# Cross-attention on one core: the first two projections and the first query-weight product in whole float32, weights in 128-column tiles from two queues

## The chip, the core and the metric

The program runs on one core of one Trainium2 chip. The metric is the device time of one execution, in microseconds (us), median of three runs. PE is TensorE, DVE is VectorE, ACT is ScalarE, POOL is GpSimd; SP is the engine whose queue issues most transfers here.

## What is computed

```python
# x [2, 2048, 512], ctx_768 [2, 77, 384]; H = 8 heads, D = 512
Q = (img_embed @ Wq).reshape(B, -1, H, D).transpose(0, 2, 1, 3)
K = (sent_embed @ Wk).reshape(B, -1, H, D).transpose(0, 2, 1, 3)
V = (sent_embed @ Wv).reshape(B, -1, H, D).transpose(0, 2, 1, 3)
score = jnp.einsum('bhqd,bhkd->bhqk', Q, K) / math.sqrt(D)
mask = (atten_mask != 0)[:, None, None, :]
score = jnp.where(mask, score, -jnp.inf)
attn = jax.nn.softmax(score, axis=-1)
ctx = jnp.einsum('bhqk,bhkd->bqhd', attn, V).reshape(B, -1, H * D)
out = ctx @ Wo + img_embed
mu = jnp.mean(out, axis=-1, keepdims=True)
var = jnp.var(out, axis=-1, keepdims=True)
return (out - mu) * jax.lax.rsqrt(var + EPS) * gamma + beta
```

All inputs are float32. The kernel never forms Q or V at full size: for every head it multiplies the query weights with the keys (Wq Kᵀ, called `a`), and the values with the output weights (V Wo, called `vw`), both on the 2 x 77 = 154 context tokens, and then works row tile by row tile of x.

## The kernel before

**Two stages.** In the first, `u` runs over 16 uses, 8 heads of keys and then 8 heads of values. `project(u)` multiplies a 384 x 512 weight block (`w_proj`, from `wk` or `wv`) with the context: four output tiles `m` of 128, each the sum of three products (k = 0 to 2). `out_product(u)` multiplies a 512 x 512 block (`w_out`, from `wq_t` or `wo`) with that result: four tiles of four products. In the second stage 32 tiles of 128 rows of x pass through scores, softmax, transposition, output product and layer norm.

**Split operands.** The matmuls run on float32r, a float32 with fewer mantissa bits. To keep precision every operand is split: ACT rounds it (`..._hi`), DVE or POOL subtracts to get the rest (`..._lo`). `short_product` then makes hi x hi and hi x lo in one 308-column matmul (`w_hi` against 2 x 154 columns), and lo x hi in one 154-column matmul. So a product costs two matmuls, and each weight block is rounded once by ACT and subtracted once by another engine: `w_proj` on POOL (line 760; use 0 alone on DVE, line 565), `w_out` on DVE (line 582). The result of a projection is evicted by ACT (`round_kv`, line 477) and split by DVE in two steps (`split_kv`, lines 598 and 602).

**Order.** Every engine has a hand-written list. PE: 8 warm-up matmuls on zeros, `project(0)`, then for each u `project(u+1)` and `out_product(u)`. From u = 10 on some out-products have transpositions of `vw_t` in their middle (line 357). ACT: ctx, w_proj of use 0 in four tiles, w_proj of use 1, then per u `round_kv(u+1)`, `round_w_proj(u+2)`, half 0 of the out-product's eviction, `round_w_out(u+1)`, half 1. DVE: ctx, w_proj of use 0, the mask bias (lines 570 and 575, from a mask that ACT's queue loads first of all), then per u `split_kv(u+1)`, half 0 of the out-product, `split_w_out(u+1)`, half 1. POOL subtracts w_proj of uses 1 to 15 and is idle else.

**Transfers.** All weights come over SP's queue in order: ctx, four 128-column tiles of use 0, two halves of use 1, then w_out(0), w_proj(2), w_out(1), gamma, beta, and on from there, each block in one transfer into a ring of three, once PE has done with the block before it in the ring. A 128-column tile of w_proj is 128 x 3 pieces of 512 bytes in memory.

Of the kernel before, what the change touches and what calls it, by code (L numbers as in the profile page):

```python
# [40 lines left out]
class Shapes:  # L41


    def __init__(self, x_tiles, ctx_t, w_proj, w_out, mask):
# [7 lines left out]
        self.dim = w_proj.shape[3]  # L52
# [26 lines left out]
def build(nc, x_tiles, x_rows, ctx_t, wk, wq_t, wv, wo, mask, gamma, beta, out):  # L79
# [5 lines left out]
    WARM_UP = 8  # L85
# [4 lines left out]
    with ExitStack() as stack:  # L90
# [54 lines left out]
        with nc.sbuf_tensor("w_out_hi0", [P, s.dim_t, s.model], F32R) as w_out_hi0, \  # L145
# [3 lines left out]
        prob = [sb("prob0", [P, s.row]), prob1]  # L149
        assert 3 * s.row <= s.dim_t * s.model  # L150
# [21 lines left out]
        ld_second = [sem(f"ld_second{n}") for n in range(2)]  # L172
# [10 lines left out]
        act_ctx_hi, act_first_hi, act_p_hi, act_o_hi = sem("act_ctx_hi"), sem("act_first_hi"), sem("act_p_hi"), sem("act_o_hi")  # L183
# [3 lines left out]
        dve_mask, dve_ctx_lo, dve_first_lo, dve_o_lo = sem("dve_mask"), sem("dve_ctx_lo"), sem("dve_first_lo"), sem("dve_o_lo")  # L187
# [41 lines left out]
        def _(sp):  # L229
# [16 lines left out]
            def load_w_proj(u):  # L246
# [570 lines left out]
```

## Time and profile before

| | us |
|---|---|
| median of 3 runs (lowest, highest) | 376.74 (375.97, 378.13) |
| the profiled execution | 375.72 |
| its span in the trace | 373.9 |
| PE busy | 360.4 |
| DVE busy | 296.0 |

The profiled execution is 1.02 us under the median, and 1.8 us of it lie outside the span. All times below count from the start of the span. An entry such as "DVE w_out_lo L582" is an operation of DVE at line 582 that writes `w_out_lo`. The start of a row is where the engine took the instruction up; a wait inside the instruction is part of its duration.

### The profile page before, as it was taken

Reading aid. Unit: us, or ns where it says so; the run is one execution under the profiler, and the core shown is the slowest. Engines: PE = TensorE matmul, PEld = TensorE weight load, DVE = VectorE, ACT = ScalarE, POOL = GpSimd, SP = SyncE. Lnnn points to the kernel's source line nnn. Section 1 sums busy time; section 2 is a strip of 40 time slices with the busy share of each in tenths; the row PEclk is TensorE's granted clock in tenths of the full one; section 3 lists DMA queues with packets and bytes.
Section 4 is the critical chain, followed back from the end, with each engine's and each line's share of the span. In section 5 each row is a group of like instructions: output and inputs, shape, how many; then the busy total and the mean of one; then the engine's idle time right before and its main releaser. Section 6 shows DMA issues by size and latency. Waiting matters only on the chain.

```text
span 373.9 us, 6759 instructions
## 1 busy us (share of the span) xinstructions
PE 360.4 (96%) x2352; PEld 335.1 (90%) x2352; DVE 296.0 (79%) x483; ACT 215.7 (58%) x750; POOL 220.9 (59%) x195
## 2 busy tenths in 40 slices
PE   6899999999999999999999999999999999999991
PEld 3899999999999998999899889988998899899880
DVE  4799999988888577777877777777778777877796
ACT  4775775777676575654565466446644654564610
POOL 0564564464338112677677757776776677667555
PEclk9999999999999999999999999999999999999997
DMA  7997768865731400314233143142241340411012
GB/s 220 389 417 283 284 242 309 339 253 203 274 141 59 169 25 34 98 74 140 88 110 140 44 156 128 43 169 85 86 140 59 140 141 30 168 66 48 30 58 84
DMA packets 20642, 55.81 MB, mean 149 GB/s; under 512 B 1664, under 2 KB 4224, under 8 KB 18560
## 3 DMA queue, kind: packets, MB, share of 16 engines
q1 hardware_dynamic: 20464, 55.29, 41.2%
q8 instruction: 19, 0.31, 0.4%
q14 instruction: 15, 0.12, 0.1%
q10 hardware_dynamic: 144, 0.08, 0.1%
HBM read 46.98 MB, written 8.39 MB: 148 GB/s over the span
## 4 chain that ended last, share of the span: by engine, by line
PE 85%; DVE 6%; POOL 3%; ACT 2%; DMA 2%; issue 1%; SPq 1%; POOLq 0%
PE pair L372 28%; PE pair L398 26%; PE pair L305 26%; PE pair L384 4%; DVE w_out_lo L582 2%; DMA w_proj<-wk 2%; PE pair L357 1%; POOL out_sb L755 1%; ACT prob L506 1%; SPq L253 1%; DVE kv_t L602 1%; POOL var_eps L744 1%; POOL centred L751 1%; ACT w_out_hi L469 1%; DVE rest L598 1%
## 5 line engine op out<-in xcount | busy, mean ns | idle before, releaser
L506 ACT ACTIVATE prob<-masked,neg_max 128x77 f32<-128x77 f32 x256 | 88.3, 347 | 100.3 <-DVE neg_max L638 100.3
L760 POOL TENSOR_TENSOR w_proj_lo<-w_proj,w_proj_hi 128x768 fp32r<-128x768 f32 x30 | 55.1, 1859 | 59.3 <-ACT w_proj_hi L461 59.3
L305 PE MATMUL pair<-kv_t,w_out_hi 128*128 128x308 f32 x256 | 66.9, 334 | 0.0
L398 PE MATMUL pair<-vw_hi,pt_hi 128*128 128x512 f32 (+1 forms) x160 | 63.2, 395 | 0.0
L398 PE MATMUL pair<-vw_lo,pt_hi 128*128 128x512 f32 (+1 forms) x160 | 63.2, 395 | 0.0
L398 PE MATMUL pair<-vw_hi,pt_lo 128*128 128x512 f32 (+1 forms) x160 | 62.5, 391 | 0.0
L372 PE MATMUL pair<-a_hi,xt_hi 128*128 128x308 f32 x256 | 59.5, 314 | 0.0
L744 POOL TENSOR_SCALAR var_eps<-mean_var 128x1 f32<-128x1 f32 x32 | 24.2, 757 | 58.8 <-DVE mean_var L676 58.5
L372 PE MATMUL pair<-a_lo,xt_hi 128*128 128x308 f32 x256 | 57.1, 304 | 0.0
L372 PE MATMUL pair<-a_hi,xt_lo 128*128 128x308 f32 x256 | 57.0, 304 | 0.0
L737 POOL TENSOR_TENSOR xt_lo<-xt_in,xt_hi 128x512 fp32r<-128x512 f32 x32 | 44.0, 1376 | 20.6 <-ACT xt_hi L498 20.6
L582 DVE TENSOR_TENSOR w_out_lo<-w_out,w_out_hi 128x1024 fp32r<-128x1024 f32 x32 | 52.9, 1691 | 2.6 <-ACT w_out_hi L469 2.2
L305 PE MATMUL pair<-ctx_split,w_proj_hi 128*128 128x308 f32 x192 | 51.4, 339 | 3.4 <-ACT w_proj_hi L450 2.4
L305 PE MATMUL pair<-kv_t,w_out_lo 128*128 128x154 f32 x256 | 52.1, 245 | 0.0
L634 DVE TENSOR_TENSOR masked<-pair,mask_bias 128x616 f32<-128x616 f32 x32 | 25.6, 799 | 29.9 <-PE pair L372 29.9
L506 ACT ACTIVATION_READ_ACCUMULATOR prob<-masked,neg_max 128x1 f32 x256 | 48.0, 187 | 0.0
L305 PEld LDWEIGHTS pair<-kv_t,w_out_lo 128*128 128x128 f32 x256 | 45.5, 190 | 0.0
L305 PEld LDWEIGHTS pair<-kv_t,w_out_hi 128*128 128x128 f32 x256 | 45.0, 190 | 0.0
L755 POOL TENSOR_TENSOR out_sb<-centred,beta_sb 128x512 f32<-128x512 f32 x31 | 40.6, 1310 | 4.4
L372 PEld LDWEIGHTS pair<-a_hi,xt_lo 128*128 128x128 f32 x256 | 42.3, 189 | 0.0
L372 PEld LDWEIGHTS pair<-a_lo,xt_hi 128*128 128x128 f32 x256 | 42.2, 188 | 0.0
L372 PEld LDWEIGHTS pair<-a_hi,xt_hi 128*128 128x128 f32 x256 | 41.4, 189 | 0.0
(54 smaller groups left out, 680.1 us busy)
## 6 DMA issues: line engine op xcount, KB each, us to landing
w_out<-wq_t SPq DMA_DIRECT2D x8, 1024.0 KB, 6.8
w_out<-wo SPq DMA_DIRECT2D x8, 1024.0 KB, 4.8
xt_in<-x_tiles SPq DMA_DIRECT2D x16, 512.0 KB, 3.7
x_in<-x_rows SPq DMA_DIRECT2D x16, 512.0 KB, 4.3
out<-out_sb SPq DMA_DIRECT2D x32, 256.0 KB, 2.1
w_proj<-wv SPq DMA_DIRECT2D x8, 768.0 KB, 5.1
w_proj<-wk SPq DMA_DIRECT2D x6, 768.0 KB, 8.2
w_proj<-wk SPq DMA_DIRECT2D x4, 192.0 KB, 4.5
```

Of the source, the lines that this page charges most:

```text
L253: sp.dma_start(tile_cols(w_proj_sb[0], m), tile_cols(src, m)).then_inc(ld_first[m], DMA_INC)
L305: mm = pe.matmul(pair[:, bank, 0:n], w[:, k, cols], moving[:, k, 0:n], start=(at == 0), stop=(at == len(steps) - 1))
L372: mm = pe.matmul(ps_scores[i % 2][:, half, 0:s.half], xs[:, k, :], a[:, k, b, half * s.half:(half + 1) * s.half], start=(k == 0 and n == 0 ...
L384: mm = pe.transpose(ps_pt[0:rows, j // 4, (j % 4) * P:(j % 4 + 1) * P], prob[i % 2][:, j * P:j * P + rows], identity[:, :])
L398: mm = pe.matmul(ps_out[:, i % 2, 0:s.model], ps[0:rows, j, :], v[0:rows, b, j, :], start=(j == 0 and n == 0), stop=(j == s.key_t - 1 and ...
L506: e = act.activation(prob[i % 2][:, cols], masked[i % 2][:, cols], ACT.Exp, bias=neg_max[i % 2][:, h:h + 1], accum_out=sums[i % 2][:, h:h ...
L582: dve.tensor_tensor(half_cols(w_out_lo[u % W_RING], half), half_cols(w_out_sb[u % W_RING], half), half_cols(w_out_hi[u % 2], half).bitcast ...
L634: dve.tensor_tensor(masked[i % 2][:, :].rearrange("p (a k) -> p a k", a=2), ps_scores[i % 2][:, :, 0:s.half], mask_bias[:, b, :].rearrange ...
L737: pool.tensor_tensor(xt_lo[i % XS_RING][:, :, :], src, xt_hi[i % XS_RING][:, :, :].bitcast(F32), ALU.subtract).then_inc(pool_xt_lo, 1)
L744: pool.tensor_scalar(var_eps[:, :], mean_var[i % 2][:, 1:2], EPS, None, ALU.add).then_inc(pool_ve, 1)
L755: pool.tensor_tensor(o, c, beta_sb[:, :], ALU.add).then_inc(pool_out, 1)
L760: pool.tensor_tensor(half_cols(w_proj_lo[u % W_RING], half), half_cols(w_proj_sb[u % W_RING], half), half_cols(w_proj_hi[u % 2], half).bit ...
```

## The change

`FULL_PROJ = 2` and `FULL_OUT = 1`: uses 0 and 1 of `project` and use 0 of `out_product` multiply float32 operands as they are, with `full_product`: one matmul of 154 columns for each product, on `w_proj_sb`, `ctx_sb`, `w_out_sb[0]` and the evicted float32 result `kv_full` (in the space of `prob1`). ACT's roundings and the subtractions on DVE and POOL for these three blocks fall away; the context is still split, for uses 2 and on. PE waits for the transfers themselves. All weights lie tile by tile in memory (128 output columns x all k together), so that a tile of w_proj is 1536 bytes in one piece per partition. Tiles 0 and 2 of uses 0 and 1 are issued on ACT's queue, tiles 1 and 3 on SP's; w_out(0) comes in two halves. The mask, gamma and beta are loaded at u = 8 instead of at the start, and DVE makes the mask bias at u = 9. There are 10 warm-up matmuls instead of 8.

```diff
-    WARM_UP = 8
+    WARM_UP = 10
+    FULL_PROJ, FULL_OUT = 2, 1
...
+            def full_product(pair, bank, w, moving, m, tiles):
+
+                for k in range(tiles):
+                    mm = pe.matmul(pair[:, bank, 0:s.toks], w[:, m, k, :], moving[:, k, 0:s.toks],
+                                   start=(k == 0), stop=(k == tiles - 1))
+                return mm
+
+            def wait_kv(u, half):
+
+                if u < FULL_OUT:
+                    pe.wait_ge(act_kv_hi, 2 * u + half + 1)
+                else:
+                    pe.wait_ge(dve_kv_lo, 2 * (u - FULL_OUT) + half + 1)
+
+            def project_full(u):
 
                 for m in range(s.dim_t):
                     half = m // 2
...
+                    pe.wait_ge((ld_first, ld_second)[u][m], DMA_INC)
+                    if m % 2 == 0 and u > 0:
+                        wait_kv(u - 1, half)
+                    mm = full_product(ps_proj[half], m % 2, w_proj_sb[u], ctx_sb, m, s.ctx_t)
+                    if m % 2:
+                        mm.then_inc(pe_proj, 1)
...
+            def out_product_full(u):
+
+                wait_kv(u, 1)
                 for m in range(s.model_t):
                     half = m // 2
                     if m % 2 == 0:
...
+                        pe.wait_ge(ld_third[half], DMA_INC)
+                    mm = full_product(ps_outp[half], m % 2, w_out_sb[u], kv_full, m, s.dim_t)
+                    if m % 2:
+                        mm.then_inc(pe_outp, 1)
...
-            act.dma_start(mask_sb[:, :], mask.rearrange("b k -> (b k)").partition_broadcast(P)).then_inc(ld_mask, DMA_INC)
...
+            for w, ld, to in ((wk[0], ld_first, w_proj_sb[0]), (wk[1], ld_second, w_proj_sb[1])):
+                for m in range(0, s.dim_t, 2):
+                    act.dma_start(tile_cols(to, m), tile_cols(w, m)).then_inc(ld[m], DMA_INC)
...
-                if u == 1:
+                if u == H:
+                    sp.dma_start(mask_sb[:, :], mask.rearrange("b k -> (b k)").partition_broadcast(P))\
+                      .then_inc(ld_mask, DMA_INC)
                     sp.dma_start(gamma_sb[:, :], gamma.partition_broadcast(P)).then_inc(ld_gamma, DMA_INC)
...
-            split_kv(0)
-            split_w_out(0)
+            split_ctx()
             for u in range(USES):
                 if u + 1 < USES:
                     split_kv(u + 1)
+                if u == H + 1:
+                    bias_of_mask()
                 if u == USES - 1:
                     mask_and_max(0)
                 take_out_product(u, 0)
```

On ACT, what stands between its table load and the rounding of w_proj(2), before:

```order
L525 ACT_TABLE_LOAD
L525 ACTIVATE ctx_split<-ctx_sb 128x3x154 [waits ld_ctx]
L450 ACTIVATE w_proj_hi<-w_proj 128x3x128 [waits ld_first0]
L450 ACTIVATE w_proj_hi<-w_proj 128x3x128 [waits ld_first1]
L450 ACTIVATE w_proj_hi<-w_proj 128x3x128 [waits ld_first2]
L450 ACTIVATE w_proj_hi<-w_proj 128x3x128 [waits ld_first3]
L461 ACTIVATE w_proj_hi<-w_proj 128x3x256 [waits ld_second0]
L461 ACTIVATE w_proj_hi<-w_proj 128x3x256 [waits ld_second1]
L477 ACTIVATE kv_t<-pair 128x2x154 [waits pe_proj] x2
L469 ACTIVATE w_out_hi<-w_out 128x4x256 [waits ld_w_out0]
L469 ACTIVATE w_out_hi<-w_out 128x4x256
L477 ACTIVATE kv_t<-pair 128x2x154 [waits pe_proj] x2
```

and now (`prob` is the buffer of `kv_full`):

```order
L495 DMA w_proj<-wk 128x384 x4
L499 ACT_TABLE_LOAD
L499 ACTIVATE ctx_split<-ctx_sb 128x3x154 [waits ld_ctx]
L523 ACTIVATE prob<-pair 128x308 [waits pe_proj] x2
L523 ACTIVATE kv_t<-pair 128x2x154 [waits pe_proj] x2
L506 ACTIVATE w_proj_hi<-w_proj 128x768 [waits ld_w_proj2]
L506 ACTIVATE w_proj_hi<-w_proj 128x768
```

Eight roundings of weights are gone from in front of the evictions, and the rounding of w_proj(2) follows the evictions of uses 0 and 1 directly.

On DVE, at u = 9, before (`rest` and `kv_t` belong to `split_kv`, `vw_t` to the eviction of the out-product):

```order
L602 SCALAR_TENSOR_TENSOR kv_t<-pair,rest 128x2x154 [waits dve_rest]
L620 TENSOR_TENSOR vw_t<-pair,vw_t 128x4x77 [waits act_vw_t]
L582 TENSOR_TENSOR w_out_lo<-w_out,w_out_hi 128x4x256 [waits act_o_hi] x2
L620 TENSOR_TENSOR vw_t<-pair,vw_t 128x4x77 [waits act_vw_t]
L598 SCALAR_TENSOR_TENSOR rest<-pair,kv_t 128x308 [waits act_kv_hi]
```

and now:

```order
L646 SCALAR_TENSOR_TENSOR kv_t<-pair,rest 128x2x154 [waits dve_rest]
L609 TENSOR_SCALAR mask_low<-mask_sb 128x154 [waits ld_mask]
L614 TENSOR_TENSOR mask_bias<-mask_low 128x1232 [waits dve_mask]
L668 TENSOR_TENSOR vw_t<-pair,vw_t 128x4x77 [waits act_vw_t]
L621 TENSOR_TENSOR w_out_lo<-w_out,w_out_hi 128x1024 [waits act_o_hi] x2
L668 TENSOR_TENSOR vw_t<-pair,vw_t 128x4x77 [waits act_vw_t]
L642 SCALAR_TENSOR_TENSOR rest<-pair,kv_t 128x308 [waits act_kv_hi]
```

The two operations of the mask bias now stand between `split_kv(10)` and the eviction of out-product 9.

## Rows read from the trace of the kernel before

**Rows 1.** Chain that ended last, from 0 to 45 us: start, us, what.
```profile
4.50 5.96 DMA w_proj<-wk
...
10.48 0.84 ACT w_proj_hi L461
11.33 0.33 ACT kv_t L477
...
11.68 0.49 DVE rest L598
...
12.19 0.49 DVE kv_t L602
...
12.82 32.19 PE pair L305 x253
```

**Rows 2.** Timeline, 0 to 21 us: start, duration, engine, line, operation, idle time before.
```profile
1.17 3.37 PE L407 MATMUL pair<-zeros 128*128 128x512 bf16 x8 [1.17 <-DVE zeros L558]
...
5.01 0.59 ACT L525 ACTIVATE ctx_split<-ctx_sb 128x462 fp32r<-128x462 f32 x1 [2.58 <-DMA ctx_sb<-ctx_t]
...
5.82 0.43 SPq L259 DMA_DIRECT2D w_proj<-wk  x1
...
6.96 0.38 PE L305 MATMUL pair<-ctx_split,w_proj_hi 128*128 128x308 f32 x1 [2.42 <-ACT w_proj_hi L450]
...
19.96 0.30 PE L305 MATMUL pair<-ctx_split,w_proj_hi 128*128 128x308 f32 x1
```

**Rows 3.** Stretches: length, busy us (instructions) of PE, PEld, DVE, ACT, POOL, clock, DMA share, GB/s.
```profile
4.00:5.00 1.00, 0.54 (x2) 0.00 (x0) 0.00 (x0) 0.00 (x0) 0.00 (x0) 1.00 1.04 309
5.00:7.00 2.00, 0.04 (x1) 0.07 (x1) 1.28 (x3) 1.64 (x3) 0.00 (x0) 1.00 1.03 296
7.00:11.00 4.00, 4.00 (x19) 4.00 (x20) 3.16 (x5) 2.41 (x4) 0.59 (x1) 0.57 1.05 372
11.00:13.00 2.00, 1.01 (x8) 0.81 (x7) 1.29 (x3) 1.10 (x4) 2.00 (x2) 1.00 1.00 420
```

**Rows 4.** DMA issues: transfer, queue, count, KB each, median us to landing; last row issued at 5.82.
```profile
w_proj<-wk SPq DMA_DIRECT2D x4, 192.0 KB, 4.5
ctx_sb<-ctx_t SPq DMA_DIRECT2D x1, 231.0 KB, 4.3
...
w_proj<-wk SPq DMA_DIRECT2D x1, 768.0 KB, 9.0
```

**Rows 5.** Chain over the whole span: PE's pieces (start, us, line, number of matmuls).
```profile
90.26 7.09 PE pair L305 x56
...
112.96 0.87 PE pair L357 x8
...
136.03 3.42 PE pair L372 x24
```

**Rows 6.** Timeline of POOL, 12 to 90 us.
```profile
17.37 3.67 POOL L760 TENSOR_TENSOR w_proj_lo<-w_proj,w_proj_hi 128x768 fp32r<-128x768 f32 x2 [3.32 <-ACT w_proj_hi L461]
...
80.97 3.67 POOL L760 TENSOR_TENSOR w_proj_lo<-w_proj,w_proj_hi 128x768 fp32r<-128x768 f32 x2 [3.40 <-ACT w_proj_hi L461]
```

**Rows 7.** Timeline of DVE around u = 9.
```profile
81.50 0.48 DVE L602 SCALAR_TENSOR_TENSOR kv_t<-pair,rest 128x308 fp32r<-128x308 f32 x1
82.22 0.48 DVE L620 TENSOR_TENSOR vw_t<-pair,vw_t 128x308 f32<-128x308 f32 x1 [0.24 <-ACT vw_t L484]
83.16 3.71 DVE L582 TENSOR_TENSOR w_out_lo<-w_out,w_out_hi 128x1024 fp32r<-128x1024 f32 x2 [0.47 <-ACT w_out_hi L469]
```

**Rows 8.** Lines 582, 575 and 570 alone: count, shortest/median/longest ns.
```profile
L582 DVE TENSOR_TENSOR w_out_lo<-w_out,w_out_hi x32: 1209/1226/2571, 14.1 to 123.5; 128x1024 fp32r<-128x1024 f32 x32
...
L575 DVE TENSOR_TENSOR mask_bias<-mask_low x1: 1442/1442/1442, 8.9 to 8.9; 128x1232 f32<-128x1232 f32 x1
...
L570 DVE TENSOR_SCALAR mask_low<-mask_sb x1: 234/234/234, 8.6 to 8.6; 128x154 f32<-128x154 int32 x1
```

**Rows 9.** Chain from 79 to 93 us.
```profile
83.16 3.71 DVE w_out_lo L582 x2
86.87 0.39 DVE vw_t L620
...
88.58 0.49 DVE kv_t L602
89.06 0.14 issue
89.20 1.06 PE pair L357 x8
```

**Rows 10.** What PE waited for over the whole span: us in total, times, longest.
```profile
PE pair L305 <- ACT w_proj_hi L450: 2.4, 1, 2.4
PE pair L407 <- DVE zeros L558: 1.2, 1, 1.2
PE pair L305 <- DVE kv_t L602: 1.0, 1, 1.0
PE pair L357 <- DVE kv_t L602: 0.8, 2, 0.4
```

More of the change, by code:

```diff
@@ L304, in short_product @@
                 for at, (w, n, k) in enumerate(steps):
-                    mm = pe.matmul(pair[:, bank, 0:n], w[:, k, cols], moving[:, k, 0:n],
+                    mm = pe.matmul(pair[:, bank, 0:n], w[:, m, k, :], moving[:, k, 0:n],
                                    start=(at == 0), stop=(at == len(steps) - 1))
                 return mm
+            def full_product(pair, bank, w, moving, m, tiles):
[6 more added lines that the diff above has]
+                    pe.wait_ge(act_kv_hi, 2 * u + half + 1)
+                else:
+                    pe.wait_ge(dve_kv_lo, 2 * (u - FULL_OUT) + half + 1)
+            def project_full(u):
+                for m in range(s.dim_t):
+                    half = m // 2
+                    pe.wait_ge((ld_first, ld_second)[u][m], DMA_INC)
[4 more added lines that the diff above has]
+                        mm.then_inc(pe_proj, 1)
             def project(u):
@@ L444, in _, with round_ctx @@
         def _(act):
[L445 to L451 removed]
+            for w, ld, to in ((wk[0], ld_first, w_proj_sb[0]), (wk[1], ld_second, w_proj_sb[1])):
+                for m in range(0, s.dim_t, 2):
+                    act.dma_start(tile_cols(to, m), tile_cols(w, m)).then_inc(ld[m], DMA_INC)
+            def round_ctx():
+                act.wait_ge(ld_ctx, DMA_INC)
+                act.activation(ctx_split[:, :, 0:s.toks], ctx_sb[:, :, :], ACT.Copy).then_inc(act_ctx_hi, 1)
             def round_w_proj(u):
+                act.wait_ge(ld_w_proj[u % W_RING], use(u - (W_RING if u % W_RING < 2 else 0), W_RING))
+                if u >= FULL_PROJ + 2:
+                    act.wait_ge(pe_proj, 2 * (u - 1))
                 for half in range(2):
[L455 to L460 removed]
                     act.activation(half_cols(w_proj_hi[u % 2], half), half_cols(w_proj_sb[u % W_RING], half),
@@ L522, in _ @@
             assert len(early_xt) == XS_RING
-            act.wait_ge(ld_ctx, DMA_INC)
-            act.activation(ctx_split[:, :, 0:s.toks], ctx_sb[:, :, :], ACT.Copy).then_inc(act_ctx_hi, 1)
-            round_first_weights()
-            round_w_proj(1)
+            round_ctx()
             round_kv(0)
-            round_w_out(0)
             for u in range(USES):
@@ L608, in take_out_product @@
                 pair = ps_outp[half]
-                if u < H:
+                if u < FULL_OUT:
+                    dve.wait_ge(act_a_hi, 2 * u + half + 1)
+                    dve.tensor_tensor(head_cols(a_lo, half, u), by_batch(first(pair)),
+                                      head_cols(a_hi, half, u).bitcast(F32), ALU.subtract).then_inc(dve_a_lo, 1)
+                elif u < H:
                     r = by_batch(next_rest()[:, :, :])
@@ L755, in scale_and_shift @@
                 pool.tensor_tensor(o, c, beta_sb[:, :], ALU.add).then_inc(pool_out, 1)
-            for u in range(1, USES):
+            for u in range(FULL_PROJ, USES):
                 for half in range(2):
-                    pool.wait_ge(act_p_hi, 2 * (u - 1) + half + 1)
+                    pool.wait_ge(act_p_hi, 2 * (u - FULL_PROJ) + half + 1)
                     pool.tensor_tensor(half_cols(w_proj_lo[u % W_RING], half), half_cols(w_proj_sb[u % W_RING], half),
```

144 lines of the change are left out of this document (74 added, 70 removed).

## The prediction

> **What bounds the kernel now.** First the table of PE's waits [rows 10]: over 373.9 us PE waits 5.4 us in all, 4.6 of them before 13 us and 0.8 at two transpositions. So from 12.82 us on PE is the bound and has next to no gap; a change of the start is worth exactly what it moves the beginning of that gapless run, and everything later keeps its distance. Then the chain's first 45 us [rows 1]: it ends in one unbroken piece of 253 matmuls from 12.82, and before it stand transfer, rounding, eviction and the two DVE steps of kv(0). The timeline [rows 2] shows PE's warm-up to 4.54, idle until 6.96 because ctx and the first tile are rounded and subtracted first, and project(2), the first product that both kernels compute alike, beginning at 19.96. That is the mark I measure against: I call it T2. Last, the stretches [rows 3]: after PE's idle 2.4 us the granted clock is 0.57 on average from 7 to 11 us, that is 3.4 us at 1.2 GHz and the rest at 2.4; before and after it is 1.00.
>
> **Part 1: when PE can start.** Ctx has landed by 5.01 [rows 2], a 192 KB tile issued behind it took 4.5 us [rows 4]. Now the first tile is issued on ACT's queue at the same time as ctx, so it lands at about 0.7 + 4.5 = 5.2; PE needs nothing more. I take 5.3 for the first product. The warm-up fills the time: 8 matmuls took 3.37 us, two more reach to 5.4 at that pace, or 5.0 at the full clock that rows 3 show from 4 us on. Either way they cost 0.1 us at most. ACT's four issues and its table load end before ctx lands. Its rounding of ctx and DVE's subtraction are needed only at T2 and are hidden by ten microseconds of matmuls.
>
> **Part 2: what a whole float32 product costs.** There is none in the trace. PE's work until T2 is 12 + 12 products of the two projections and 16 of the out-product, 40 products of price f, so T2 = 5.3 + 40 f if nothing else is late. A split product is two matmuls: 56 in 7.09 us are 127 ns each, 0.253 for the pair of 308 and 154 columns. A 308-column matmul alone takes 3.42 / 24 = 0.142 and a 128-column transposition of float32 0.87 / 8 = 0.109 [rows 5], so a 154-column one takes 0.253 - 0.142 = 0.111, about as long as the transposition although it has 26 columns more: at this size a matmul is held up by its weights, not its columns. The lower bound for f is one such pass, 0.11. The upper bound is four of them, each with its own weights, 0.444. The exact product of two operands of two parts has four partial products of 154 columns, 616 columns; the split one leaves lo x lo out and has 462. I take the value of two 308-column matmuls, 2 x 0.142 = 0.284: the weights have two parts, and the columns of both parts of the moving operand follow each. Then T2 = 5.3 + 11.4 = 16.7.
>
> **Part 3: the other road to T2, the data of w_proj(2).** It lands at 5.82 + 9.0 = 14.8 before [rows 2, 4]. Ahead of it in the queues are the same blocks without the mask. The 768 KB of use 0 moved at about 300 GB/s in 512-byte pieces, where later stretches show 372 and 420 [rows 3]: in pieces of 1536 bytes that is worth some 0.6 us; the mask 0.2; two queues issuing at once in the first microseconds perhaps 0.5. So it lands at about 13.5, in any case between 12.5 and 14.8. Behind it stand one rounding half (0.84, rows 1) and one subtraction on POOL (3.67 / 2 = 1.84, rows 6) plus 0.2 of signals: T2 is not before 13.5 + 2.9 = 16.4, with the ends 15.4 and 17.7. The two roads are 0.3 us apart, PE's the later. The second half of POOL is needed 1.5 us after T2 and comes 1.8 us after the first, covered by the 0.3 between them, or costing 0.3 where PE is the earlier.
>
> Between 5.3 and T2 the other waits are short of PE: ctx and use 0 (1 MB) have landed by about 6.3, use 1 by 8.4, needed tile by tile from 8.7 on; w_out(0) by 11, needed at 12.1; the eviction of kv(0), 0.43, sits under the other half's matmuls. w_out(1) lands by 16.4, is rounded and subtracted by 20, and is needed half by half at 19.8 and 21.8. Gamma and beta, 512 KB, leave the busy stretch, so w_proj(3) comes 3 us sooner and stays off the path. **Gain at the start: 19.96 - 16.7 = 3.3 us**, between 4.6 (PE's road short, data early) and a loss of 3.1 (f = 0.444, T2 = 23.1).
>
> **Part 4: the mask bias at u = 9.** At the start it lay where DVE had time; its removal there is worth nothing. At u = 9 it stands in a DVE list on which PE waits: the chain from 79 to 93 us runs w_out_lo, vw_t, split_kv(11) on DVE up to 89.06, and PE's transpositions start at 89.20, 0.4 late [rows 9, 10]. The cost alone is 0.23 + 1.44 = 1.67 us [rows 8]. DVE is free from 81.97 to 82.22 and 82.69 to 83.16 [rows 7], and inside its w_out_lo something is idle too: 32 of them have a median of 1.23 and a longest of 2.57 [rows 8]. The pair from 83.16 takes 3.71, and it ends at 86.87, that is 2.23 (two short ones) after POOL's pair, 80.97 to 84.64, has ended [rows 6, 7]. So a DVE operation that reads two SBUF tensors stands still while POOL's runs; those that read PSUM (the 0.48 rows) don't. The mask bias reads SBUF twice. It is taken up at 82.0, in the middle of POOL's pair, and stands until 84.64, then needs 1.3 to 1.4 and ends at 86.1; vw_t 0.4, w_out_lo 2 x 1.13, vw_t 0.4, split_kv(11) 1.8 end at 91.1 instead of 89.06. **Loss: 2.1 us**, all of it on PE, since its transpositions already wait. Half 0 of out-product 10 is late by 1.2 of these 2.1 already at its own start. If nothing stood still, 1.67 us would end at 83.7, vw_t at 84.1, and w_out_lo would still begin after POOL at 84.6: loss 0. If mask bias slips in between POOL's two operations, POOL's second is late in its place, 1.6 to 2.1.
>
> The rule for this is in the Trainium skill, "SBUF — State Buffer", its section on the shared port pair: DVE with two SBUF inputs and a GpSimd operation hold one port pair exclusively, whoever starts second fully blocks. It speaks against this move, and the 2.57 beside 1.21 agree with it; a reader of the Trainium skill alone would also charge about 2 us here, against 0 without the rule.
>
> On part 2 the Trainium skill, "FP8 and Floating Point Precision", section "TensorE Precision Notes", says that true float32 takes four passes through the array. No run so far shows it. Taken as four passes of columns it gives T2 = 16.7, as four passes with weights each, T2 = 23.1.
>
> **The sum.** 373.9 - 3.3 + 2.1 = 372.7 span, 374.5 for the profiled execution, which lay 1.0 under the median: on the median's scale 376.74 - 1.2 = **375.5 us**.
>
> **Rivals.** (a) The mask bias costs nothing, because it is not stopped or finds its place: 376.74 - 3.3 = 373.4. For it: it is short of the idle time of DVE around 82 to 84.6. Against: rows 8. Chance 0.15. (b) PE's clock falls in the first products, as it did after the idle 2.4 us: 3.4 us at 1.2 instead of 2.4 GHz cost 1.7, T2 = 18.4, time 377.2. Against it: there is hardly an idle time left, from 5.4 on PE is busy. A late first tile would bring it. The same time comes from f = 0.32, or from w_proj(2) landing at 15. Chance together 0.2. (c) Slower: each of the four partial products loads weights of its own, f = 0.444. The place is the 40 products before T2, the price 40 x 0.16 = 6.4 us over my forecast, time 381.9. It decides against the change from f = 0.314 on, where 40 f has eaten the 1.2 us. For it: a 154-column matmul is bound by its weights today. Chance 0.12. (d) The change doesn't shorten the start because the transfers come no sooner than before: T2 = 17.7, time 376.5, chance 0.08. My forecast has 0.45.
>
> **Range and chances.** A measurement tells about 0.5% (1.9 us) from no change. Faster by more than that needs (a), or both a cheap product and early data with w_proj(2) at 12.5 (T2 = 15.6, time 374.4): 0.28. Slower: (c) and the far end of (b): 0.15. Within: 0.57. The range leaves out (c) above and only the best of (a) with early data below: 372.2 to 378.4.
>
> **What would show it.** In the trace of the changed kernel: the first matmul on ctx_sb at 5.2 to 5.5; 12 of them in 3.4 us (1.3 would be one pass, 5.3 four with weights); the first matmul on ctx_split at 16.7, released by PE's own list, not by POOL; a clock of 1.00 from 4 us on; mask_bias as a DVE row much longer than 1.44, at 78 to 82 us, ending with POOL's pair plus 1.4; the transpositions after it waiting 2.5 instead of 0.4. Wrong is the forecast if f lies over 0.31, or if the mask bias shows 1.44 with PE's wait unchanged.

## The result, and the profile after

The changed kernel takes **373.91 us**, the median of 6 runs (373.74 to 374.21), against 376.01 us (375.52 to 378.13) for 6 runs of the kernel before: a ratio of 0.9942, 95% interval 0.9922 to 0.9962. It is 0.6% faster, 2.1 us by the medians. The forecast was 375.5 us, 1.2 under the median shown then. Of 53 later runs of the kernel before, 45 lie between 375.3 and 376.4 and 8 between 377.7 and 378.7, and one of the latter kind was among the three that the forecast had. The two profiled executions are 1.5 us apart: their spans are 373.9 and 372.4, their times 375.7 and 374.2.

The forecast had two terms, 3.3 gained before T2 and 2.1 lost at u = 9. Three marks test them (us from the start of the span, each from the profiled execution):

| | first product | T2 | transpositions after u = 9 | from T2 to there | from there to the end |
|---|---|---|---|---|---|
| before | 6.96 | 19.96 | 89.20 | 69.24 | 284.7 |
| after | 5.42 | 16.53 | 87.71 | 71.18 | 284.7 |
| difference | -1.54 | -3.43 | -1.49 | +1.94 | 0.0 |

The start is the timeline of the kernel after, 0 to 22 us (start, duration, engine, line, operation, idle time before), the counterpart of [rows 2]:

```profile
1.17 4.45 PE L448 MATMUL pair<-zeros 128*128 128x512 bf16 x10 [1.17 <-DVE zeros L600]
...
5.42 6.51 PE L320 MATMUL pair<-ctx_sb,w_proj 128*128 128x154 f32 x48
...
11.77 4.36 PE L320 MATMUL pair<-prob,w_out 128*128 128x154 f32 x32
...
14.45 3.64 POOL L809 TENSOR_TENSOR w_proj_lo<-w_proj,w_proj_hi 128x768 fp32r<-128x768 f32 x2 [12.96 <-ACT w_proj_hi L506]
...
16.53 0.38 PE L313 MATMUL pair<-ctx_split,w_proj_hi 128*128 128x308 f32 x1 [0.40 <-POOL w_proj_lo L809]
```

PE goes from warm-up to the end of the first out-product without a gap. A whole float32 product shows as two matmul records: 24 products in x48, 16 in x32. From 5.42 to the end of the second group, 16.13, are 10.71 us, which is 0.268 for each of the 40 products where 0.284 was forecast. Then PE waits 0.40 for POOL. The chain of the kernel after (start, us, what) shows the road that ended last there:

```profile
3.99 9.44 DMA w_proj<-wk
...
13.46 0.85 ACT w_proj_hi L506
...
14.45 1.83 POOL w_proj_lo L809
...
16.53 23.48 PE pair L313 x183
```

The stretches of the kernel after (length, busy us and instructions of PE, PEld, DVE, ACT, POOL, granted clock, DMA share, GB/s) are the counterpart of [rows 3]:

```profile
4.00:7.00 3.00, 3.00 (x16) 2.23 (x15) 0.64 (x1) 0.56 (x1) 0.00 (x0) 1.00 1.07 386
7.00:11.00 4.00, 4.00 (x33) 4.00 (x32) 0.15 (x1) 1.28 (x3) 0.00 (x0) 1.00 0.98 339
11.00:17.00 6.00, 5.60 (x43) 5.39 (x42) 1.29 (x3) 3.37 (x6) 2.55 (x2) 1.00 1.03 433
```

The clock of 0.57 from 7 to 11 us in [rows 3] is gone. And the chain of the kernel after around u = 9, with its table of PE's waits (us in total, times, longest), is the counterpart of [rows 9, 10]:

```profile
78.76 0.96 DVE mask_low L609
...
79.75 2.98 DVE mask_bias L614
82.73 0.39 DVE vw_t L668
83.12 2.27 DVE w_out_lo L621 x2
...
87.58 0.14 issue
87.71 1.07 PE pair L398 x8
```

```profile
PE pair L398 <- DVE kv_t L646: 1.4, 2, 1.0
PE pair L448 <- DVE zeros L600: 1.2, 1, 1.2
PE pair L313 <- DVE w_out_lo L621: 1.0, 1, 1.0
PE pair L313 <- POOL w_proj_lo L809: 0.4, 1, 0.4
```

The two operations of the mask bias, 0.23 and 1.44 when alone [rows 8], take 0.96 to 1.04 and 2.98 here, and PE pays: 1.0 more at `w_out_lo`, 0.6 more at the transpositions. Not all of the 1.94 in the table above is theirs: e1 and e3 below make the mask bias at the start and still need 69.46 and 69.42 us from T2 to the transpositions, 0.2 more than before. Where these 0.2 come from stays open. The mask bias costs the other 1.7.

### The profile page after: what moved, and what is told of

It reads as the page before. It is cut to its first block, busy times and chain, and to the rows that moved or that the text cites. A ratio compares the mean times of both kernels' runs of the same rounds, so it can differ in the third digit from the quotient of the medians.

```text
span 372.4 us, 6736 instructions
## 1 busy us (share of the span) xinstructions
PE 360.4 (97%) x2354; PEld 334.6 (90%) x2354; DVE 288.5 (77%) x469; ACT 210.2 (56%) x742; POOL 217.8 (58%) x193
## 4 chain that ended last, share of the span: by engine, by line
PE 82%; DVE 8%; POOL 3%; DMA 3%; ACT 2%; issue 1%; SPq 1%; POOLq 0%
PE pair L413 28%; PE pair L439 26%; PE pair L313 22%; PE pair L425 4%; DVE w_out_lo L621 3%; DMA w_proj<-wk 3%; PE pair L398 1%; POOL out_sb L804 1%; DVE mask_bias L614 1%; DVE kv_t L646 1%; ACT prob L552 1%; POOL var_eps L793 1%; DVE rest L642 1%; ACT w_out_hi L514 1%; POOL centred L800 1%
## 5 line engine op out<-in xcount | busy, mean ns | idle before, releaser
L809 POOL TENSOR_TENSOR w_proj_lo<-w_proj,w_proj_hi 128x768 fp32r<-128x768 f32 x28 | 51.9, 1877 | 61.0 <-ACT w_proj_hi L506 61.0
L313 PE MATMUL pair<-kv_t,w_out_hi 128*128 128x308 f32 x240 | 62.8, 335 | 1.0 <-DVE w_out_lo L621 1.0
L621 DVE TENSOR_TENSOR w_out_lo<-w_out,w_out_hi 128x1024 fp32r<-128x1024 f32 x30 | 48.9, 1668 | 2.8 <-ACT w_out_hi L514 2.4
L313 PE MATMUL pair<-kv_t,w_out_lo 128*128 128x154 f32 x240 | 48.9, 245 | 0.0
L313 PE MATMUL pair<-ctx_split,w_proj_hi 128*128 128x308 f32 x168 | 43.9, 332 | 0.4 <-POOL w_proj_lo L809 0.4
L313 PEld LDWEIGHTS pair<-kv_t,w_out_hi 128*128 128x128 f32 x240 | 42.2, 190 | 1.2 <-issue 1.2
L313 PEld LDWEIGHTS pair<-kv_t,w_out_lo 128*128 128x128 f32 x240 | 42.6, 190 | 0.0
```

The costliest lines, as they stand in the source:

```text
L313: mm = pe.matmul(pair[:, bank, 0:n], w[:, m, k, :], moving[:, k, 0:n], start=(at == 0), stop=(at == len(steps) - 1))
L621: dve.tensor_tensor(half_cols(w_out_lo[u % W_RING], half), half_cols(w_out_sb[u % W_RING], half), half_cols(w_out_hi[u % 2], half).bitcast ...
L809: pool.tensor_tensor(half_cols(w_proj_lo[u % W_RING], half), half_cols(w_proj_sb[u % W_RING], half), half_cols(w_proj_hi[u % 2], half).bit ...
```

## The experiments

In what follows "the mask at the start" means that it is loaded on ACT's queue and DVE makes the bias before anything of u = 0. Spans and marks are of the profiled executions, one of each kernel. They scatter: the kernel after and e6 have the same code and transfers up to T2, and their T2 are 16.53 and 15.93. The medians and intervals carry the verdicts; each ratio is to the kernel before, run beside the variant on the same chip. e9 to e11 ran on another chip than e1 to e8, the kernel before there at 376.17.

### e1: the late mask undone

```diff
-                    sp.dma_start(mask_sb[:, :], mask.rearrange("b k -> (b k)").partition_broadcast(P))\
-                      .then_inc(ld_mask, DMA_INC)
...
                     act.dma_start(tile_cols(to, m), tile_cols(w, m)).then_inc(ld[m], DMA_INC)
+            act.dma_start(mask_sb[:, :], mask.rearrange("b k -> (b k)").partition_broadcast(P)).then_inc(ld_mask, DMA_INC)
...
             split_ctx()
+            bias_of_mask()
...
-                if u == H + 1:
-                    bias_of_mask()
```

> The changed kernel, but with the mask loaded at the start (on ACT's queue, behind its four weight tiles) and the mask bias made by DVE at the start, behind the context's subtraction, where DVE waits anyway. Theory (the mask bias at u = 9 stands still behind POOL and costs 1.9 us of PE): the transpositions of out-product 10 wait 0.4 us as in the kernel before, T2 (first matmul of project(2)) stays at 16.5 to 16.8, the time falls by 1.8 to 2.0 to about 372.1 us, ratio 0.990. Rival (the mask bias costs nothing, the start's gain is lost elsewhere): 374.0.

Measured: 372.53 us (372.31 to 373.26) against 375.99, ratio 0.9896 (0.9862 to 0.9931). Two pieces of its chain, and its row of waits for the transpositions:

```profile
16.62 23.47 PE pair L311 x183
...
86.08 1.07 PE pair L396 x8
```

```profile
PE pair L396 <- DVE kv_t L645: 0.9, 2, 0.4
```

T2 is 16.62, the transpositions begin at 86.08 and wait 0.4 as before, and nothing waits for `w_out_lo`. From T2 to the transpositions are 69.46 us, 0.2 over the 69.24 of before. So the start is worth 3.3 to 3.4 us by the marks, and placing the mask at u = 9 gives back 1.4 (medians) to 1.7 (spans) of it. This kernel beats both.

### e2: the late mask alone

```diff
+                if u == H:
+                    sp.dma_start(mask_sb[:, :], mask.rearrange("b k -> (b k)").partition_broadcast(P))\
+                      .then_inc(ld_mask, DMA_INC)
...
-            act.dma_start(mask_sb[:, :], mask.rearrange("b k -> (b k)").partition_broadcast(P)).then_inc(ld_mask, DMA_INC)
...
                 if u + 1 < USES:
                     split_kv(u + 1)
+                if u == H + 1:
+                    bias_of_mask()
```

> The kernel before with this one part of the change: mask loaded at u = 8, mask bias made by DVE at u = 9, between split_kv(10) and the eviction of out-product 9. Gamma and beta stay where they were. Theory: 1.9 to 2.1 us slower than before, about 378.0, mask_low and mask_bias 0.8 and 1.5 us longer than at the start. Rival: no difference, 376.0.

Measured: 379.84 us (379.03 to 380.27), ratio 1.0086 (1.0053 to 1.0119). From T2 to the transpositions are 71.00 us, 1.76 more than before, as the theory said. `mask_bias` shows 3.00. But the kernel is 1.8 us slower than expected, and that comes from the start: T2 is 21.70 instead of 19.96. The table of waits and the stretches of this kernel:

```profile
PE pair L308 <- DVE kv_t L605: 1.9, 1, 1.9
```

```profile
11.00:13.00 2.00, 0.10 (x2) 0.06 (x1) 1.13 (x3) 1.12 (x3) 2.00 (x2) 1.00 1.00 416
...
14.00:16.00 2.00, 2.00 (x11) 2.00 (x10) 1.68 (x2) 1.67 (x3) 0.22 (x1) 0.51 0.99 410
16.00:19.00 3.00, 3.00 (x20) 3.00 (x20) 2.19 (x5) 1.13 (x3) 0.00 (x0) 0.76 1.04 345
```

Without the mask beside it, the context landed 2.7 us after its issue (4.3 before [rows 4]), and the first product began at 5.36, 1.6 earlier. But w_proj(1) came no sooner, so PE stood longer before it: next to nothing from 11 to 13 us, then a clock of 0.51 from 14 to 16. From the end of that gap to T2 PE takes 8.74 us (12.96 to 21.70), before 7.14 (12.82 to 19.96) for the same matmuls. Starting early without data behind it lost 1.7 us.

### e3: whole products with the old transfers

```diff
-        return w.reshape(w.shape[0] // P, P, heads, dim // P, P).transpose(2, 1, 3, 0, 4)
+        return w.reshape(w.shape[0] // P, P, heads, dim).transpose(2, 1, 0, 3)
...
-                    for m in range(1, s.dim_t, 2):
+                    for m in range(s.dim_t):
...
-                    for m in range(1, s.dim_t, 2):
-                        sp.dma_start(tile_cols(w_proj_sb[1], m), tile_cols(src, m)).then_inc(ld_second[m], DMA_INC)
+                    for half in range(2):
+                        sp.dma_start(half_cols(w_proj_sb[1], half), half_cols(src, half))\
+                          .then_inc(ld_second[half], DMA_INC)
...
-            for w, ld, to in ((wk[0], ld_first, w_proj_sb[0]), (wk[1], ld_second, w_proj_sb[1])):
-                for m in range(0, s.dim_t, 2):
-                    act.dma_start(tile_cols(to, m), tile_cols(w, m)).then_inc(ld[m], DMA_INC)
+            act.dma_start(mask_sb[:, :], mask.rearrange("b k -> (b k)").partition_broadcast(P)).then_inc(ld_mask, DMA_INC)
```

The edit is against the kernel after. The layout, the pieces and the one queue are those of before. W_out(0) comes whole, gamma and beta at u = 1, and the mask is at the start.

> Whole float32 products for uses 0 and 1 of the projection and use 0 of the out-product, but the weights in the old layout, in the old pieces and all on SP's queue, with mask, gamma and beta at the start as before. Theory (T2 is set by the landing of w_proj(2) plus rounding and subtraction): it lands at 14.8 as before, T2 = 17.9, gain 2.1 us, time 373.9. Rival (the transfers don't matter, PE's road of 40 products sets T2): T2 = 5.7 + 10.4 + 0.3 = 16.4, time 372.4.

Measured: 373.55 us (373.14 to 373.91), ratio 0.9924 (0.9897 to 0.9951). That is level with the kernel after, although T2 is later. First product 5.89, T2 17.42. Three rows of its timeline:

```profile
5.89 6.53 PE L318 MATMUL pair<-ctx_sb,w_proj 128*128 128x154 f32 x48 [0.43 <-DMA w_proj<-wk]
...
14.36 1.58 ACT L502 ACTIVATE w_proj_hi<-w_proj 128x768 fp32r<-128x768 f32 x2 [1.47 <-DMA w_proj<-wk]
...
17.42 0.38 PE L311 MATMUL pair<-ctx_split,w_proj_hi 128*128 128x308 f32 x1 [0.39 <-POOL w_proj_lo L804]
```

With the old transfers, whole products bring T2 forward by 2.54 us of the 3.43. The other 0.9 come with the new transfers: w_proj(2) has landed by 13.43 in the kernel after and 14.34 here. The cleaner comparison is e1, which differs from this kernel in the transfers alone: T2 0.8 apart (16.62 and 17.42), the medians 1.0 (372.53 and 373.55).

### e4 and e7: the new transfers with split products

```diff
-                    for m in range(s.dim_t):
+                    for m in range(1, s.dim_t, 2):
...
+            for w, ld, to in ((wk[0], ld_first, w_proj_sb[0]), (wk[1], ld_second, w_proj_sb[1])):
+                for m in range(0, s.dim_t, 2):
+                    act.dma_start(tile_cols(to, m), tile_cols(w, m)).then_inc(ld[m], DMA_INC)
             act.dma_start(mask_sb[:, :], mask.rearrange("b k -> (b k)").partition_broadcast(P)).then_inc(ld_mask, DMA_INC)
```

This is the kernel before with the new layout, the tiles of w_proj(0) and w_proj(1) on two queues, w_out(0) in halves, and gamma and beta at u = 8. The mask stays at the start in e4, on ACT's queue behind the four tiles.

> All products split as before, but the weights tile by tile, from two queues, w_out(0) in two halves, gamma and beta at u = 8; mask at the start. Theory: the first matmul comes at 6.1 instead of 6.96, project(1) 1.4 us sooner, T2 = 18.5, gain 1.4 us, time 374.6; with e3's 2.1 it adds up to the 3.4 of the changed kernel. Rival (the transfers alone give nothing, since rounding and POOL hold the start): 376.0.

e4 measured: 379.59 us (378.89 to 380.37), ratio 1.0085 (1.0057 to 1.0113), where 374.6 was expected. The table of waits, DVE's timeline and the stretches of e4:

```profile
PE pair L309 <- DVE kv_t L613: 5.2, 1, 5.2
```

```profile
10.01 0.90 DVE L581 TENSOR_SCALAR mask_low<-mask_sb 128x154 f32<-128x154 int32 x1 [2.29 <-DMA mask_sb<-mask]
...
10.95 2.97 DVE L586 TENSOR_TENSOR mask_bias<-mask_low 128x1232 f32<-128x1232 f32 x1
```

```profile
12.00:13.00 1.00, 0.00 (x0) 0.00 (x0) 1.00 (x1) 0.90 (x2) 0.62 (x1) 0.58 1.05 440
13.00:14.00 1.00, 0.00 (x0) 0.00 (x0) 1.00 (x2) 0.47 (x1) 0.00 (x0) 0.50 1.03 434
...
16.00:19.00 3.00, 3.00 (x16) 3.00 (x14) 2.36 (x3) 0.43 (x1) 0.00 (x0) 0.50 1.03 432
```

Queued behind four weight tiles, the 77 KB of the mask took 7.4 us and landed at 9.98. The mask bias stands in DVE's list ahead of `split_kv(0)`, which PE waits for, and DVE could begin it only then, while POOL ran (8.99 to 12.62). Both operations came to their stretched durations, PE stood 5.2 us, and its next matmuls ran at half the clock. So e4 measured the place of the mask, not the transfers. In e1 the same load is hidden, because there `split_kv(0)` doesn't exist and nothing of the first 16 us waits for DVE. e7 asks the question again, with the mask out of the start:

```diff
+                if u == H:
+                    sp.dma_start(mask_sb[:, :], mask.rearrange("b k -> (b k)").partition_broadcast(P))\
+                      .then_inc(ld_mask, DMA_INC)
...
-            act.dma_start(mask_sb[:, :], mask.rearrange("b k -> (b k)").partition_broadcast(P)).then_inc(ld_mask, DMA_INC)
...
+                if u == H + 1:
+                    bias_of_mask()
                 if u + 1 < USES:
                     split_kv(u + 1)
```

> All products split as before, weights tile by tile from two queues, w_out(0) in two halves, mask, gamma and beta at u = 8, mask bias at the top of u = 9. The mask no longer stands in front of kv(0) on DVE, which is what held e4_split_new_transfers. Theory: first product at about 5.9, project(1) at 11, T2 at 18.0 with a full clock, 19.7 if PE's idle time in front of project(1) is followed by a half-clock stretch: 374.1 or 375.8. Rival (the slow e4 run came from the transfers): 379 again.

e7 measured: 374.71 us (374.29 to 376.27, 12 runs), ratio 0.997 (0.9952 to 0.9989). T2 is 18.25 and the transpositions begin at 88.19. So with split products the new transfers, with the mask out of their way, are worth 1.7 us at T2, and the late mask in its better place takes back 0.7 (69.94 to the transpositions against 69.24). The two halves of the change overlap: 2.5 with the one and 1.7 with the other make 3.4 together. What taking out the mask adds to the 1.7 was not measured by itself with these transfers; with the old ones it made T2 later (e2).

### e5: a third projection whole

```diff
-    FULL_PROJ, FULL_OUT = 2, 1
+    FULL_PROJ, FULL_OUT = 3, 1
...
-                    pe.wait_ge((ld_first, ld_second)[u][m], DMA_INC)
+                    if u < 2:
+                        pe.wait_ge((ld_first, ld_second)[u][m], DMA_INC)
+                    elif m == 0:
+                        pe.wait_ge(ld_w_proj[u], DMA_INC)
...
-                if u + 2 < USES:
+                if FULL_PROJ <= u + 2 < USES:
```

The rest is e1's.

> e1_mask_start with use 2 of the projection also in whole float32 (FULL_PROJ = 3), so that project(2) waits for neither ACT nor POOL. Theory (PE's road and POOL's road to T2 are 0.3 to 0.6 us apart, and a whole product costs 0.261 us against 0.253): project(2) starts at 16.1 instead of 16.6 and takes 0.1 longer, time 0.3 to 0.5 us under e1_mask_start, about 372.1. Rival (w_proj(3) or w_out(1) becomes the next late one): no gain, 372.5 or more.

Measured: 372.20 us (371.61 to 372.6), ratio 0.9891 (0.9862 to 0.992), 0.33 under e1, which is within the scatter of either. Its chain shows what it was to show, and no wait for POOL is left:

```profile
1.17 4.45 PE pair L449 x10
5.62 14.00 PE pair L318 x104
19.62 20.43 PE pair L311 x162
```

104 records are 52 products in 14.00 us: 0.269 each. The third projection in the timeline of e5:

```profile
16.31 3.31 PE L318 MATMUL pair<-ctx_sb,w_proj 128*128 128x154 f32 x24
```

It starts at 16.31, where e1 starts it at 16.62, and project(3) follows at 23.48 instead of 23.89. So the same work takes 7.17 us here and 7.27 in e1: twelve whole products were no dearer in this place than twelve split ones. The gain of 0.4 is still there at the transpositions (85.67 and 86.08) and agrees with the 0.33 of the medians.

### e6: the mask bias one place earlier

```diff
+                if u == H + 1:
+                    bias_of_mask()
                 if u + 1 < USES:
                     split_kv(u + 1)
-                if u == H + 1:
-                    bias_of_mask()
```

> The changed kernel with the two mask operations one place earlier in DVE's list: at the top of u = 9, before split_kv(10) instead of behind it. Same work, same transfers. There POOL's pair of u = 9 has not begun (it starts about 0.9 us after ACT's eviction of the second half). Theory (what costs is standing still behind POOL, not the 1.67 us of work): mask_low 0.23 and mask_bias 1.44 as alone, they end before POOL does, w_out_lo starts no later, PE's transpositions wait 0.4 us again, time 372.0, like the kernel with the mask at the start. Rival (any 1.67 us in this chain costs its length): 373.9, as the changed kernel.

Measured: 372.48 us (372.31 to 372.7), ratio 0.9899 (0.9871 to 0.9928), 1.4 under the kernel after. Four rows of its timeline, DVE's and POOL's:

```profile
76.26 0.22 DVE L609 TENSOR_SCALAR mask_low<-mask_sb 128x154 f32<-128x154 int32 x1
...
76.52 1.44 DVE L614 TENSOR_TENSOR mask_bias<-mask_low 128x1232 f32<-128x1232 f32 x1
...
77.15 4.32 POOL L809 TENSOR_TENSOR w_proj_lo<-w_proj,w_proj_hi 128x768 fp32r<-128x768 f32 x2 [3.42 <-ACT w_proj_hi L506]
...
80.06 3.63 DVE L621 TENSOR_TENSOR w_out_lo<-w_out,w_out_hi 128x1024 fp32r<-128x1024 f32 x2
```

Here `mask_bias` begins 0.6 us before POOL. It takes its 1.44 us, and now POOL's pair is the one that stands: 4.32 instead of 3.67 [rows 6]. So the stall goes either way, to whoever comes second. And it comes back to DVE: `w_out_lo` is taken up at 80.06, stands until POOL's late pair ends at 81.47, and ends 2.22 us after it (2.23 before). From T2 to the transpositions are 70.09 us, 0.63 more than e1's 69.46, where the theory had 0: what POOL lost, 0.65. In the kernel after it is 1.72 over e1's. e7 and e9 have the mask bias in the same place and repeat it. POOL's pair at u = 9 takes 4.37 in e7 and 4.33 in e9; the row of e7:

```profile
79.26 4.37 POOL L775 TENSOR_TENSOR w_proj_lo<-w_proj,w_proj_hi 128x768 fp32r<-128x768 f32 x2 [3.40 <-ACT w_proj_hi L470]
```

That is 0.70 and 0.66 over 3.67, and from T2 to the transpositions both kernels lose 0.70 and 0.65 against before.

The start of e6 is the same code as that of the kernel after, but PE doesn't wait for POOL in it:

```profile
5.30 6.46 PE L320 MATMUL pair<-ctx_sb,w_proj 128*128 128x154 f32 x48
11.60 4.36 PE L320 MATMUL pair<-prob,w_out 128*128 128x154 f32 x32
15.93 0.38 PE L313 MATMUL pair<-ctx_split,w_proj_hi 128*128 128x308 f32 x1
```

ACT takes up w_proj(2) at 12.86, 0.6 sooner than in the kernel after, and PE's own list comes last. T2 at 15.93 is 0.7 before e1's, which loads the mask at the start, and the medians of e6 and e1 are the same (372.48 and 372.53). So the mask's early place at u = 9 costs about what its absence from the start gives.

### e8: is the gain only warm-up?

```diff
-    WARM_UP = 8
+    WARM_UP = 10
```

This is the kernel before with nothing else changed.

> The kernel before with 10 warm-up matmuls instead of 8, nothing else. Theory (where the half-clock stretch falls decides: in the kernel before it lies over project(0), whose time the landing of use 1 covers; with less idle time ahead of it project(0) runs at the full clock, ends sooner, and the idle time in front of project(1) grows from 1.3 to over 2 us and halves the clock behind it, where nothing covers it): project(1) still starts at 12.8, T2 at 21.6, time 377.7. Rival (the clock's stretch costs nothing in either place): 376.0.

Measured: 376.16 us (375.65 to 378.5, 12 runs), ratio 1.0011 (0.9991 to 1.0031). T2 is 19.92. Two more matmuls of warm-up do nothing by themselves. The slowdown that I had expected of it did not come either, because its premise did not hold: project(0) ran no faster behind the longer warm-up. Two stretches of e8:

```profile
7.00:9.00 2.00, 1.93 (x8) 1.96 (x9) 1.92 (x5) 1.05 (x2) 0.00 (x0) 1.00 1.09 365
...
13.00:16.00 3.00, 3.00 (x25) 3.00 (x25) 2.47 (x4) 2.25 (x3) 1.02 (x1) 1.00 0.96 397
```

From 7 to 9 us 8 matmuls pass, from 13 to 16 us 25, over 8 in each microsecond. That is half the pace, and yet the granted-clock column shows 1.00 in both. Early in a trace this column alone doesn't tell the pace of PE; the number of matmuls does.

### e9: e2 with the better place of the mask bias

```diff
+                if u == H + 1:
+                    bias_of_mask()
                 if u + 1 < USES:
                     split_kv(u + 1)
-                if u == H + 1:
-                    bias_of_mask()
```

> e2_mask_late_only with the two mask operations at the top of u = 9, where e6_bias_before_split_kv showed them to cost nothing. What is left of the change is that the mask isn't loaded at the start. Theory (the mask's late place costs 1.9 us; the other 1.9 us of e2 come from the start: without the mask's transfer ctx lands 1.6 us sooner, project(0) ends sooner, PE idles 2.2 us in front of project(1) and works at the half clock for 3.4 us behind it): 377.9, T2 at 21.7 again. Rival (e2's whole loss comes from u = 9): 376.0, T2 at 20.0.

Measured: 378.66 us (377.98 to 379.6, 10 runs), ratio 1.0059 (1.0039 to 1.0078), 1.18 under e2 (1.36 when each is taken against the kernel before on its own chip). From T2 to the transpositions are 69.89, 0.65 more than before, where e2 had 1.76: the same 1.1. The expectation had e6's place down as free; it costs these 0.65. Its start is e2's code, and in this execution it went worse still, T2 at 22.68 where 21.7 was expected. Its table of waits and its stretches:

```profile
PE pair L308 <- DVE kv_t L605: 2.8, 1, 2.8
```

```profile
11.00:13.00 2.00, 0.16 (x1) 0.19 (x2) 1.26 (x3) 1.00 (x4) 2.00 (x2) 0.71 0.98 411
13.00:14.00 1.00, 1.00 (x5) 1.00 (x6) 0.56 (x2) 1.00 (x2) 0.40 (x1) 0.50 1.04 434
14.00:16.00 2.00, 2.00 (x10) 2.00 (x10) 1.92 (x2) 0.99 (x2) 0.00 (x0) 0.50 0.98 414
```

The gap in front of project(1) is 2.8 us and the clock is at half from its last part on. From the gap's end to T2 PE takes 9.84 us (12.84 to 22.68), before 7.14. So in the kernel before, the later start of the first product was not a loss: project(0) lay closer to the data of project(1).

### e10 and e11: three whole projections and the better place

```diff
-    FULL_PROJ, FULL_OUT = 2, 1
+    FULL_PROJ, FULL_OUT = 3, 1
```

This is e6 with e5's edit. E11 has beside it:

```diff
-    WARM_UP = 10
+    WARM_UP = 8
```

> e6_bias_before_split_kv with FULL_PROJ = 3: mask loaded at u = 8, bias at the top of u = 9, three projections in whole float32. Theory: as e5_full_three_projections, but without the mask's 77 KB in the first transfers: 372.0. Rival: no different from e6, 372.5.

> e10_three_proj_bias_moved with 8 warm-up matmuls instead of 10. Theory (ctx and the first tile have landed by 5.0, the warm-up holds PE to 5.4 when the full clock is granted late; behind it PE's road alone sets T2 now): 0.2 to 0.4 us less, 371.7. Rival (a gap of 0.5 us in front of the first product costs the clock, or nothing is gained since the first tile lands at 5.0 to 5.4): 372.0 or up to 373.7.

Measured: e10 372.31 us (371.74 to 372.69), ratio 0.9884 (0.986 to 0.9908); e11 372.16 us (371.5 to 372.74), ratio 0.9881 (0.9857 to 0.9905). With 8 warm-up matmuls the first product starts at 4.77 instead of 5.62, by their chains, but the 104 records then take 14.66 us instead of 13.91 and end at 19.43 instead of 19.53. The first of them pass more slowly: 7 between 6 and 7 us, where e10 has 9, again with 1.00 in the clock column. The row of e11's first two projections:

```profile
4.56 7.52 PE L320 MATMUL pair<-ctx_sb,w_proj 128*128 128x154 f32 x48
```

The next group starts at 11.92, 7.36 us later, where e6 needs 6.30 for the same 24 products. The medians of e1, e5, e6, e10 and e11 all lie between 372.1 and 372.6 and are not told apart by these runs. The interval of each lies below 0.9942, the ratio of the kernel after.

## Why the prediction was right, and where its steps were off

The forecast of 375.5 lies 1.6 us above the measured median, inside its range; the sign was right, the size short. By its own steps:

**The reading of the bound held.** In all thirteen kernels the distance from the transpositions after u = 9 to the end of the span is 284.6 or 284.7 us. A change of the start is worth what it moves the gapless run of PE, to a tenth of a microsecond.

**Part 1, when PE can start:** 5.3 forecast, 5.42 measured. The ten warm-up matmuls took 4.45 us, 0.427 us from one weight load to the next (2.00 to 4.56 in six steps) at 512 columns. That is the pace of 1.2 GHz all the way, although the granted-clock column shows 1.00. Of the two ends that the prediction gave, the slow one was right.

**Part 2, the price of a whole product:** 0.284 forecast, 0.268 measured (10.71 / 40). The term was over-sized by 40 x 0.016 = 0.65 us. Without the ends of the stretch it is a little less still: e6's two projections, 24 products from 5.30 to 11.60, take 0.262 each, 4% more than the 0.253 of a split pair [rows 5]. The reason given, two matmuls with weights of two parts, agrees with the two matmul and two weight records of each product. These records, the kernel after's line 320 alone (count, shortest, median and longest ns, first and last start):

```profile
L320 PEld LDWEIGHTS pair<-ctx_sb,w_proj x48: 187/190/338, 5.0 to 11.5; 128*128 128x128 f32 x48
L320 PE MATMUL pair<-ctx_sb,w_proj x48: 292/294/350, 5.4 to 11.6; 128*128 128x154 f32 x48
```

That the columns of both parts pass in each of the two is not shown by the records; it is what a time of 0.131 each (0.262 / 2), next to 0.142 for 308 columns and 0.111 for 154, suggests.

On this point the Trainium skill, "FP8 and Floating Point Precision", section "TensorE Precision Notes", has true float32 as four passes through the array. The records and the 0.268 fit four passes of columns under two weight loads; they do not fit four with weights each (T2 = 23.1 in the prediction, rival c).

**Part 3, the other road:** w_proj(2) landed at 13.43, 13.5 forecast, and the road through ACT and POOL ended at 16.53, 16.4 forecast. PE's own list ended at 16.13, where 16.7 was forecast, since part 2 was over-sized. So in this execution POOL's road came last, and "released by PE's own list, not by POOL" failed. That T2 still moved by 3.43 where 3.3 stood is partly luck: T2 is the later of two roads some 0.4 apart, and the second stood in for the first. Nor is the order fixed: in e6, with the same start, PE's list came last.

**Part 4, the mask bias:** 2.1 forecast. The forecast's own steps behind 86.1 (0.4, 2 x 1.13, 0.4 and 1.8) add up to 90.96 and not 91.1, so they give 1.9. Measured are 1.94 between the marks, of which 1.7 are the mask bias (1.72 over e1 in the kernel after, 1.76 over before in e2). Of the three cases given, the first occurred: `mask_bias` was taken up at 79.75, stood until POOL's pair ended at 81.43 (77.75 plus 3.68), and ended at 82.73, 1.30 after it, where 1.3 to 1.4 was forecast. In front of it `mask_low` stood too, until 0.1 after the first of POOL's two operations. The two didn't delay POOL, whose pair took 3.68. What was not foreseen is where PE pays: 1.0 at `w_out_lo` and 0.6 at the transpositions, instead of all of it at the transpositions.

The Trainium skill, "SBUF — State Buffer", section "SBUF: two separate sides", has a DVE operation with two SBUF inputs and a GpSimd operation that reads SBUF contend for one port pair: it goes to whoever starts first for the whole instruction, and the other blocks. Here 2.98 against 1.44 agrees, and so does e6's reverse, POOL's 4.32 against 3.67. What it doesn't give is the price of one place or the other: 1.7 and 0.65.

**The sum.** On spans: forecast -1.2, measured -1.5, of which 0.13 from the start and 0.16 from u = 9. **The scale:** on medians -2.1 was measured, to 373.9 and not 375.5. Of these 1.6 us, 0.7 is the starting point (376.74 in the forecast, 376.01 in the comparison), 0.3 the two terms, and 0.6 lies in which executions were profiled: that of before is 0.3 under its median of 376.01, that of after 0.3 over its own. The prediction took its profiled execution for 1.0 under the median and carried that on.

**The rivals.** (a), a mask bias that costs nothing, fell: e1 shows what it would have given, 372.5. (b), a clock that falls in the first products, did not occur in the kernel after: its 24 first products took 6.35 us (5.42 to 11.77), 0.265 each, beside 0.262 in e6. A small part of it shows in e1, e5 and e10, where they took 6.6 to 6.7, and in e11, 7.36: there the first matmuls on the context passed more slowly (in e11 6 and 7 in the microseconds from 5 and from 6 us, and 10 in the next). It is real where PE gets a gap, as e2, e4 and e9 show, at 1.6 to 2.7 us. (c) fell with f = 0.268, and (d) with w_proj(2) at 13.43.

## What to carry to other kernels

Where a small first stage waits for operands to be rounded and subtracted, whole float32 products at 154 columns cost about 4% more of PE (0.262 against 0.253 us) and take the rounding and subtracting off the path. That was worth 2.5 of 374 us. An operation "moved to where DVE has time" needs a look at POOL in the same microseconds. The same 1.67 us of work cost nothing that shows at the start of e1, where nobody waited for DVE, 0.65 at one place of u = 9 and 1.7 one `split_kv` later; in e4's start, in front of what PE needed next, they made PE stand for 5.2 us. And an earlier start is only worth what its data can sustain: e2 and e9 began 1.5 us sooner and reached T2 1.7 and 2.7 us later.

## What the runs showed of the hardware that was not expected

- A whole float32 product of 128x128 by 154 columns is two matmul and two weight records. It takes 0.262 us in an even run (e6), 0.268 and 0.269 with the ends of the stretch (after, e5).
- A DVE operation with one SBUF input also stands behind POOL: `mask_low`, 128x154, int32 in and float32 out, took 1.04 us instead of 0.23 (after) and 0.90 (e4), ending 0.10 us after POOL's operation both times. The prediction had reckoned with this only for two inputs.
- The mask, 77 KB in flight beside the first transfers, delays them: the context landed after 4.3 us with it (before, e8) and after 2.7 and 2.6 without (e2, e9). Issued behind four tiles on the same queue it took 7.4 us itself (e4), 4.5 as the queue's first.
- After a gap of PE, the same 7.14 us of matmuls took 8.74, 9.01 and 9.84 us (e2, e4, e9), with the clock granted at half for part of it.
- The granted-clock column can read 1.00 while PE passes matmuls at half the pace: 8 from 7 to 9 us in e8, against 25 from 13 to 16.
- Who stands between DVE and POOL is decided by who comes first, and the delay travels: 1.44 us of `mask_bias` begun 0.6 us ahead of POOL made POOL's pair 0.65 longer (e6; 0.70 in e7, 0.66 in e9), and the next DVE operation with two SBUF inputs stood until that pair had ended.
